# Neighbour search of a four-layer graph network: z in two fp32r parts, squares split in column form

## What is computed

```python
h = relu(layernorm(x))
z = leaky_relu(lap_mul(A, h) @ W1 + b1, 0.1)         # 4096 x 128
sq = sum(z * z, axis=-1)
d2 = max(sq[:, None] + sq[None, :] - 2 * (z @ z.T), 0)
S = exp(-sqrt(d2 + 1e-10) / 2)                       # 4096 x 4096
S = where(rank of S in its row < 4, S, 0)            # the four nearest neighbours
out = lap_mul(S + A, h) @ W2 + b2                    # lap_mul scales by 1/sqrt(row sums) on both sides
```

## Time and profile before

| | us |
|---|---|
| median of three runs | 1520.61 (1513.95 to 1523.7) |
| the profiled execution, whole time | 1512.57 |
| its span in the profile | 1510.7 |
| first MAX8 starts | 927.03 |
| last FIND_INDEX8 ends | 1279.00 |
| last indirect DMA issued, end | 1502.05 |

### The profile page before, as it was taken

How to read it: one execution, slowest core, us unless ns; L and a number is a source line. 1 busy time by engine, 2 the same in 40 slices (tenths; PEclk the granted TensorE clock), 3 DMA queues, 4 the chain that set the end, 5 groups by cost and what they waited for, 6 DMA issues and landing times.

```text
span 1510.7 us, 15178 instructions
## 1 busy us (share of the span) xinstructions
PE 1424.8 (94%) x5244; PEld 886.5 (59%) x5244; DVE 1210.1 (80%) x1617; ACT 789.4 (52%) x1111; POOL 176.1 (12%) x177
## 2 busy tenths in 40 slices
PE   7999999999999999999989898999999999879993
PEld 4556677787788677777776672222222223666672
DVE  7987888889998887665589995788888888577883
ACT  2312233357666776655576653444444444576863
POOL 0000000000000000000000000000000000687886
PEclk9999999999999999999999999999999999989997
DMA  8777665568767756665587790000000003979992
GB/s 329 243 263 225 220 207 188 191 222 297 263 223 237 278 192 213 209 195 181 173 315 259 262 340 16 0 7 7 7 7 1 7 7 110 371 271 365 384 348 86
DMA packets 82859, 291.46 MB, mean 193 GB/s; under 512 B 10848, under 2 KB 10976, under 8 KB 82784
## 3 DMA queue, kind: packets, MB, share of 16 engines
q1 hardware_dynamic: 78048, 280.01, 53.9%
q0 software_dynamic: 4736, 10.49, 2.2%
HBM read 286.27 MB, written 4.19 MB: 192 GB/s over the span
## 4 chain that ended last, share of the span: by engine, by line
PE 67%; DVE 14%; POOL 11%; issue 5%; ACT 2%; DMA 1%; SPq 0%; POOLq 0%; ACTq 0%; DVEq 0%
PE ps L581 18%; POOL landing L1225 10%; PE ps L413 9%; PE ps L415 9%; PE ps L414 9%; PE ps L418 8%; DVE A_lo L1041 7%; PE ps L582 5%; PE ps L486 1%; PE ps L514 1%; PE ps L515 1%; POOL picks L1222 1%; PE ps L455 1%; DVE hn L895 1%; PE ps L449 1%
## 5 line engine op out<-in xcount | busy, mean ns | idle before, releaser
L1041 DVE TENSOR_TENSOR A_lo<-ring,A_hi 128x1024 fp32r<-128x1024 f32 x426 | 502.7, 1216 | 67.2 <-ACT A_hi L619 65.9
L619 ACT ACTIVATE A_hi<-ring 128x1024 fp32r<-128x1024 f32 x426 | 437.8, 1055 | 146.5 <-PE ps L415 120.1
L413 PE MATMUL ps<-A_hi,G_odd_hi 128*128 128x512 f32 x716 | 294.7, 412 | 30.9 <-DVE A_lo L1041 30.9
L581 PE MATMUL ps<-in_b 128*128 128x512 f32 x512 | 289.6, 648 | 4.6 <-DVE colsum L1031 4.6
L415 PE MATMUL ps<-A_hi,G_odd_lo 128*128 128x512 f32 x716 | 283.5, 396 | 0.0
L414 PE MATMUL ps<-A_lo,G_odd_hi 128*128 128x512 f32 x716 | 283.0, 395 | 0.0
L619 ACT ACTIVATE scores<-ps,neg_sq 128x2048 f32<-128x2048 f32 x64 | 126.0, 1968 | 196.2 <-PE ps L582 196.2
L1114 DVE MAX8 rows_T<-scores 128x8 f32<-128x4096 f32 x32 | 141.7, 4427 | 63.8 <-ACT scores L619 63.8
L413 PEld LDWEIGHTS ps<-A_hi,G_odd_hi 128*128 128x128 f32 x716 | 136.7, 191 | 78.0 <-issue 38.6
L1225 POOL DMA_INDIRECT landing<-scaled_rows,picks x128 | 158.3, 1237 | 39.5 <-issue 31.3
L1215 POOL DMA_DIRECT2D scaled_rows<-G_last x8 | 6.2, 780 | 1280.1 <-ACT G_last L619 1280.1
(11 more groups left out here) (132 smaller groups left out, 1209.4 us busy)
## 6 DMA issues: line engine op xcount, KB each, us to landing
ring<-adj_t SPq DMA_DIRECT2D x524, 512.0 KB, 4.7
X<-x_rows SPq DMA_DIRECT2D x8, 256.0 KB, 7.4
scaled_rows<-G_last POOLq DMA_DIRECT2D x8, 256.0 KB, 2.7
landing<-scaled_rows,picks POOLq DMA_INDIRECT x128, 5.5
out_rows<-X SPq DMA_DIRECT2D x8, 256.0 KB, 6.2
pack<-packed SPq DMA_DIRECT2D x1, 836.0 KB, 14.4
pack<-packed SPq DMA_DIRECT2D x1, 192.0 KB, 4.0
```

What stands on the lines that cost most here:

```text
L413: mm(acc, G_hi[odd][:, kb, t, :], hi, start=start, stop=False)
L581: mm(ps[:, bank_of(c), :], zt, in_b[:, c, :], start=True, stop=False)
L619: return nc.scalar.activation(out_ap, in_ap, func, **k)
L1041: v_.tensor_tensor(A_lo[:, s, :, :], ring[:, s, :, :], A_hi[:, slot_of(v), :, :].bitcast(fp32), ALU.subtract).then_inc(lower_ready, 1)
```

## The change

It touches the last layer's search and the steps that feed it.

- z transposed is kept in two fp32r parts: `z_hi` (ACT, in the memory of `in_b`) and `z_lo` (DVE, new step `z_rest`, in the memory of `G_even_hi`).
- In the search each half is now four bf16 matmuls (one in each bank, which open the accumulation) and then, bank by bank, three fp32r matmuls: hi by hi, hi by lo, lo by hi.
- The squares are split into three bf16 parts in column form, on 128 x 4 elements, and `square_row` turns them into rows by four bf16 matmuls of 128 columns with a bf16 identity; ACT's new step `aug_out` copies the 3 x 512 result to `sq_aug`. The fp32 matmul of line 535, ACT's second pass of `z_out` and the seven DVE instructions on 3 x 512 go.
- The due times of the last layer's chain are earlier and closer, and `z_out` comes ahead of `squares`.
- `scores0` moves into the memory of `A_hi`, `scores1` stays; ACT waits, before the splits of the second pass, for all scans but the last.

```diff
-    3: (("DVE", "add_out", 3.3), ("ACT", "move_out", 6.3), ("PE", "natural", 6.3), ("DVE", "lap_rows", 9.5),
-        ("PE", "z_transposes", 12.0), ("ACT", "squares", 15.3), ("ACT", "z_out", 15.3), ("PE", "square_row", 17.5),
-        ("DVE", "square_parts", 21.0)),
+    3: (("DVE", "add_out", 0.3), ("ACT", "move_out", 0.3), ("PE", "natural", 1.8), ("DVE", "lap_rows", 3.0),
+        ("PE", "z_transposes", 5.5), ("ACT", "z_out", 6.5), ("ACT", "squares", 7.0), ("DVE", "z_rest", 7.2),
+        ("DVE", "square_parts", 9.0), ("PE", "square_row", 11.0), ("ACT", "aug_out", 12.0)),
...
+        z_lo = at("z_lo", [P, NB, BLK], r32, even)
+        scores = [at("scores0", [P, N], fp32, hi_at), at("scores1", [P, N], fp32, even + 16384)]
...
+        z_hi = at("z_hi", [P, NB, BLK], r32, b_at)
+        A_hi = at("A_hi", [P, STAGED, UK, BLK], r32, hi_at)
...
             def square_row(b):
-                pe.wait_ge(z2_ready, nth_in(3, b))
+                pe.wait_ge(sqparts_ready, nth_in(3, b))
...
-                mm(ps[0:3, GB, :], halves[:, :], hTs[:, :], start=True, stop=True).then_inc(sqrow_full, 1)
+                for n in range(TPB):
+                    last = mm(ps[0:3, GB, n * P:(n + 1) * P], sq_parts[:, n, :], ident16[:, :], start=True, stop=True)
+                last.then_inc(sqrow_full, 1)
...
-            def pair_columns(t, c):
-                zt = in_b[:, t // TPB, t % TPB * P:(t % TPB + 1) * P]
-                mm(ps[:, bank_of(c), :], zt, in_b[:, c, :], start=True, stop=False)
-                return mm(ps[:, bank_of(c), :], ones3[:, :], sq_aug[:, c, :], start=False, stop=True)
+            def pair_columns(t, cs):
+
+                at_row = t % TPB * P
+                hi, lo = (z[:, t // TPB, at_row:at_row + P] for z in (z_hi, z_lo))
+                for c in cs:
+                    mm(ps[:, bank_of(c), :], ones3[:, :], sq_aug[:, c, :], start=True, stop=False)
+                for c in cs:
+                    mm(ps[:, bank_of(c), :], hi, z_hi[:, c, :], start=False, stop=False)
+                    mm(ps[:, bank_of(c), :], hi, z_lo[:, c, :], start=False, stop=False)
+                    last = mm(ps[:, bank_of(c), :], lo, z_hi[:, c, :], start=False, stop=True)
+                last.then_inc(half_full, 1)
...
             def z_out(b):
                 act.wait_ge(zT_full, nth_in(3, b))
-                f(in_b[:, b, :], ps[:, TB, :], ACT.Copy)
-                act.wait_ge(sqrow_full, rank[3, b])
-                f(hTs[:, :], ps[:, TB, :], ACT.Square).then_inc(z2_ready, 1)
+                f(z_hi[:, b, :], ps[:, TB, :], ACT.Copy).then_inc(zhi_ready, 1)
+
+            def aug_out(b):
+                act.wait_ge(sqrow_full, nth_in(3, b))
+                f(sq_aug[:, b, :], ps[0:3, GB, :], ACT.Copy).then_inc(aug_ready, 1)
...
             scale_last(m - 1)
+            act.wait_ge(scanned, NT - 1)
             for j, v in enumerate(PLAN.visits[PLAN.rows_end:]):
...
+            def z_rest(b):
+
+                dve.wait_ge(zhi_ready, nth_in(3, b))
+                v_.tensor_tensor(z_lo[:, b, :], ps[:, TB, :], z_hi[:, b, :].bitcast(fp32),
+                                 ALU.subtract).then_inc(zlo_ready, 1)
+
             def square_parts(b):
...
-                own.add(v_.tensor_copy(part_hi[:, :], row))
...
+                v_.tensor_scalar(neg_sq[:, TPB * b:TPB * (b + 1)], sq_cols[:, :], -1.0, None,
+                                 ALU.mult).then_inc(negsq_ready, 1)
+                half, rest = sq_rest[:, 0, :], sq_rest[:, 1, :]
+                own.add(v_.tensor_scalar(half, sq_cols[:, :], -0.5, None, ALU.mult))
+                own.settle()
+                own.add(v_.tensor_copy(sq_parts[:, :, 0], half))
+                own.settle()
+                own.add(v_.tensor_tensor(rest, half, sq_parts[:, :, 0], ALU.subtract))
+                own.settle()
+                own.add(v_.tensor_copy(sq_parts[:, :, 1], rest))
+                own.settle()
+                v_.tensor_tensor(sq_parts[:, :, 2], rest, sq_parts[:, :, 1], ALU.subtract).then_inc(sqparts_ready, 1)
```

More of the change, by code:

```diff
@@ L204, in gnn_stack @@
         even, odd_at, ring_at = take("area_even", 32), take("area_odd", 32), take("area_ring", 4 * SLOTS)
-        a_at, b_at = take("area_a", 16), take("area_b", 16)
+        a_at, b_at, hi_at = take("area_a", 16), take("area_b", 16), take("area_hi", 4 * STAGED)
         G_hi = [at("G_even_hi", [P, NB, TPB, P], r32, even), at("G_odd_hi", [P, NB, TPB, P], r32, odd_at)]
@@ L210, in gnn_stack @@
                 at("G_odd_lo", [P, NB, TPB, P], r32, odd_at + 16384)]
-        scores = [at(f"scores{n}", [P, N], fp32, even + 16384 * n) for n in range(2)]
+        z_lo = at("z_lo", [P, NB, BLK], r32, even)
+        scores = [at("scores0", [P, N], fp32, hi_at), at("scores1", [P, N], fp32, even + 16384)]
         near = at("near", [P, TPB, P], fp32, even)
@@ L245, in gnn_stack @@
         sq_aug = colsum[0:3, :, :].bitcast(bf16).rearrange("p t (b n) -> p (t b) n", n=BLK)
-        part_hi = sb("part_hi", [3, BLK], bf16)
-        part_mid = sb("part_mid", [3, BLK], bf16)
-        rest = sb("rest", [3, BLK])
+        sq_cols = sb("sq_cols", [P, TPB])
+        sq_parts = sb("sq_parts", [P, TPB, 3], bf16)
+        sq_rest = sb("sq_rest", [P, 2, TPB])
+        ident16 = sb("ident16", [P, P], bf16)
         ones3 = sb("ones3", [3, P], bf16)
-        halves = sb("halves", [P, 3])
         ones = sb("ones", [P, 1])
@@ L290, in gnn_stack @@
             sem("rz_full"), sem("rz_ready"), sem("n_full"), sem("t_ready"), sem("n_ready"), sem("u_ready"))
-        z_ready, zT_full, z2_ready, sqrow_full, aug_ready = (
-            sem("z_ready"), sem("zT_full"), sem("z2_ready"), sem("sqrow_full"), sem("aug_ready"))
+        z_ready, zT_full, zhi_ready, zlo_ready = sem("z_ready"), sem("zT_full"), sem("zhi_ready"), sem("zlo_ready")
+        sqparts_ready, sqrow_full, aug_ready = sem("sqparts_ready"), sem("sqrow_full"), sem("aug_ready")
         half_full, half_out, scanned = sem("half_full"), sem("half_out"), sem("scanned")
@@ L442, in natural @@
                 elif p == 3 and rank[p, b]:
-                    pe.wait_ge(z2_ready, rank[p, b])
+                    pe.wait_ge(zlo_ready, rank[p, b])
                 elif p == 3:
@@ L586, in pair_rows @@
                     pe.wait_ge(half_out, 2 * i + half - 1)
-                    for c in columns[4 * half:4 * half + 4]:
-                        last = pair_columns(seek[i], c)
-                    last.then_inc(half_full, 1)
+                    pair_columns(seek[i], columns[4 * half:4 * half + 4])
             def first_pairs(cs):
@@ L594, in first_pairs @@
                     pe.wait_ge(aug_ready, nth_in(3, c))
-                    last = pair_columns(seek[0], c)
-                last.then_inc(half_full, 1)
+                    pe.wait_ge(zlo_ready, nth_in(3, c))
+                pair_columns(seek[0], cs)
             last_row = seek_blocks[-1]
@@ L762, in step @@
                     candidate(b)
+                elif name == "z_out":
+                    z_out(b)
                 else:
-                    z_out(b)
+                    aug_out(b)
             def first_rectify(b):
@@ L1064, in step @@
                     lap_rows(b)
+                elif name == "z_rest":
+                    z_rest(b)
                 else:
@@ L1090, in _ @@
             dve.wait_ge(rest_loaded, 16)
+            v_.tensor_copy(ident16[:, :], ident)
             v_.tensor_tensor(gate_bias[:, :], pack[:, 16 * P + C_IR:16 * P + C_IR + 2],
@@ L1205, in _ @@
             g.memset(ones3[:, :], 1.0)
-            g.memset(halves[:, :], -0.5)
             g.memset(ones[:, :], 1.0)
```

23 lines of the change are left out of this document (6 added, 17 removed).

## The result

The changed kernel takes 1436.0 us (median of four, 1433.8 to 1436.4) against 1520.7 before (median of four, 1514.0 to 1523.7): a ratio of 0.947 (0.944 to 0.950). The forecast was 1443 (1426 to 1468).

A forecast was written before the change was run, and what follows sets the result against it. PE was taken to bound the search, DVE the last layer's rows. Gains of 56.8 + 10 + 6 + 0.8 = 73.6 us gave 1439.0 from the profiled execution, 1447.0 from the median; the middle, 1443 us, was predicted (1426 to 1468).

The forecast's parts named there:

- The new bound: Search: DVE becomes the bound at 8.95 us a scan, with PE at 7.5 us a row; gain 56.8 us.
- The hand-over: Search, banks passed between PE and ACT: DVE doesn't wait for scores; PE pauses about 1.5 us in each row.
- The rows: Last layer's rows, 788 to 903.6 us: less work for DVE and PE; gain 10 us (−3 to 16).
- DVE's relief: Last layer's rows: DVE does 1.7 in place of 4.5 us per block, 19.6 us less over seven blocks.
- the closer due times might cost something: Last layer's rows: with less lead for PE, stalls could eat all the gain or cost 3 us more than before.
- The last chain: Last block, from last visit to first MAX8: MAX8 at 921.1 in place of 927.03; gain 6 us (4 to 8).
- The end: After the scans: `similarity` no longer behind a split of ACT, gathers stay at 209 us; gain 0.8 us (−4 to 4).
- ACT would be free before the last scan ends: End of the search: four splits released one scan before the end leave ACT free for `similarity`; part of 0.8 us gain.
- Rival (a): Search: PE's short pauses lower its clock; at one and a half low stretches a row, 1475 us; chance 10 in 100.
- Rival (c): Search: fp32r matmuls run at double pitch, 0.46 us, a row takes 13.0 us, 1559 us in all; chance 3 in 100.

The follow-up runs named there:

- Half the scan: The changed kernel with MAX8 and FIND_INDEX8 over only the first 2048 of 4096 scores: 1397.6 us in one execution.
- a fourth product: The changed kernel with a fourth fp32r matmul, lo by lo, added in each chunk of the search: 1461.4 us in one execution.
- one product: The changed kernel with only the hi by hi fp32r matmul left in each chunk of the search: 1435.3 us in one execution.
- the two kernels that exchange split and due times: The changed kernel with the old split of the squares and new due times, 1455.2 us; with the new split and old due times, 1432.2 us.
- the interleaved kernel: The changed kernel with each bf16 matmul directly ahead of its own bank's three fp32r ones: 1597.9 (profiled), 1549.5, 1687.5 and 1472.9 us.
- the two kernels without pauses: The changed kernel scanning only the first 2048 scores, 1397.6 us, and the changed kernel with a lo by lo matmul added per chunk, 1461.4 us.

## Why the prediction was right, and where not

**The sum.** The profiled execution took 1436.3 us, where the terms gave 1439.0: scans 4.6 and rows 1.2 us better, chain 0.9 and end 2.3 worse. The other 4 us of 1443 come from the choice of a value between the profiled execution and the median before.

**The new bound.** Right, mechanism and size. Half the scan gave PE's 7.89 us a row, a fourth product cost 0.62 of 1.84 us, one product gained nothing. The term was 56.8, measured 61.4: I had 8.95 us a scan from the last one of the trace before, and in a stream it is 8.85; the small steps, too, overlap the scans' ends and cost less than the sum of their durations.

**The hand-over.** Right in what counts: DVE waited for ACT only before the first scan (9.7 us). PE's pauses were misplaced: not 1.5 us in every row, but 0.9 to 2.6 us in every second one, such as this:

```profile
1150.48 1.03 PE L588 MATMUL ps<-colsum,ones 3*128 3x512 bf16 x4 [2.46 <-ACT scores L628]
```

ACT's steps for `similarity` and the roots were put at some 2 us; the trace before has 3.3 us for them, 2 x 1.28 of it table loads.

**The rows.** 10 forecast, 11.2 measured. The step "DVE's relief" is shown by the two kernels that exchange split and due times. That the closer due times might cost something, the lower bound of this term, has no support beyond 2.6 us.

**The last chain.** 6 forecast, 5.1 measured, step by step as worked out: `z_out` at 898.1, `aug_out` at 901.7, low clock after it; the half behind it took 6.3 us (902.31 to 908.58) in place of 5.75. The prediction's sentence that no engine is busy in this stretch misreads: PE is, for 16.95 of 23.4 us, and what is serial is the order of the steps. Moving `squares` back under PE's chunks brought `aug_out` 0.7 us forward, from 9.3 to 8.5 us behind the last visit, but the half behind it then took 6.7 us, and 18.3 became 18.0 only.

**The end.** +0.8 forecast, −1.5 measured. The step that ACT would be free before the last scan ends was wrong: ACT's last split starts at 1200.52 and ends 0.2 us after the scans, since it waits for its unit from HBM, not for the scans.

```profile
1200.52 1.06 ACT L628 ACTIVATE A_hi<-ring 128x1024 fp32r<-128x1024 f32 x1 [0.19 <-DMA ring<-adj_t]
```

The store still came 1.1 us earlier behind the scans, near the 0.8 of the forecast. The gathers took 209.5 us where they took 207.6 before, first to last start, which is within what they vary by from profile to profile.

**Rival (a), the clock.** I gave it 10 in 100 on the ground that a slow PE has no pause, and that without pauses the clock comes back. That ground was wrong, although the rival didn't come: in the interleaved kernel PE ran for 300 us without a pause at 1.2 GHz. What protects the changed kernel is its order, the four three-row matmuls first, which before the experiments looked like a matter of 0.1 us per change of type. The short pauses that the rival was about cost next to nothing: the clock of the search is 0.97, and the scans take 290.6 to 290.7 us in every kernel that is bound by DVE and scans all scores. The Trainium skill ("TensorE: Matmul & The Clock Gate", "A second HAM failure mode: psum-queue depth-cycling") tells of a clock that goes back and forth where PE idles briefly between groups of matmuls. The trace agrees that it does, about once in six rows (five stretches of 3.4 us); it stays at 1.00 in the two kernels without pauses. But rival (a) needed more than one low stretch a row for its 1475 us, and here the few there are lie under DVE's work.

**Rival (c)**, fp32r at a double pitch, fell: 0.23 us at full clock. At the low clock with nothing but the order changed, a kernel of just this kind did come out at 1550 to 1690 in three of four executions: a slow PE was a real danger, by the clock and not by the pitch that this rival names.

## To carry to other kernels

When an engine is relieved, work out the next one's own time per round from its start-to-start distances: here DVE's 9.0 us against PE's 7.5 gave the gain within 5 us. Put matmuls on few rows together and let full ones follow in a long run: spread evenly, one to three full ones, they held TensorE at half its clock here though it never paused. And look at several executions: the interleaved order gave 1473 us once, and 1688 another time.

## What was not expected of the hardware

- A three-row bf16 matmul between 128-row fp32r ones costs about 0.29 us more per chunk than its 0.23 at full clock (1.21 against 0.92); a bf16 matmul on 128 rows in the same place costs nothing extra. With a three-row fp32r one a chunk is longer still (2.30 against 2.11 us, both at 1.2 GHz).
- At 1.2 GHz a search in which every fourth matmul, evenly spread, has three rows stays there: 300 us in the profiled interleaved kernel, the whole search in the one with fp32r (0.50 over 570 us). With as many full as three-row matmuls, in groups of four and with pauses, it stays there too (0.50 over 260 us), at no price, as DVE was the bound. With four three-row ones and then twelve full ones it rose again 7 us after it fell, and with one three-row one to each fp32 one after 10 us.
- Taking 20.9 us of copies and waits out of POOL's chain gave 8.7 us there (209.5 to 200.8, where unchanged gathers vary from 205.7 to 212.2); the gaps between indirect DMAs grew in their place.
